# Routing pieces of an attention and mixture-of-experts kernel: spread over more steps, moved from VectorE to GpSimd, with GpSimd's row operations left at 128x1024

## The reference, cut to what matters

```
h = layernorm(x) * (1 + ca) + sa
x = x + ga * attention(h)                     # full softmax attention, rotary q and k
h = layernorm(x) * (1 + cb) + sb
logits = silu(h @ rw1 + rb1) @ rw2 + rb2      # the router: 8 logits per token
w = softmax over the two largest logits, 0 elsewhere
x = x + gb * (h + sum_e w[e] * (silu(h @ we1[e] + be1[e]) @ we2[e] + be2[e]))
```

## Time and profile before

| | us |
|---|---|
| median of 3 runs (lowest, highest) | 1129.0 (1128.48, 1135.22) |
| the profiled execution, its own time | 1136.76 |
| its span, first to last instruction | 1134.9 |
| busy in the span: PE, DVE, ACT, POOL | 922.2, 832.1, 730.0, 301.4 |
| granted TensorE clock, mean | 0.893 |

### The profile page before, as it was taken

How to read it: one execution, slowest core, us unless ns; L and a number is a source line. 1 busy time by engine, 2 the same in 40 slices (tenths; PEclk the granted TensorE clock), 3 DMA queues, 4 the chain that set the end, 5 groups by cost and what they waited for, 6 DMA issues and landing times. The chain is left out here.

```text
span 1134.9 us, 17714 instructions
## 1 busy us (share of the span) xinstructions
PE 922.2 (81%) x5990; PEld 370.1 (33%) x5990; DVE 832.1 (73%) x1159; ACT 730.0 (64%) x1576; POOL 301.4 (27%) x447
## 2 busy tenths in 40 slices
PE   2363569999998998999898999979978869987692
PEld 1232012222222222222222222312312159986682
DVE  3885989999998967999897789897682017443275
ACT  0033028888887875888687788869568846654361
POOL 1332000000001601400160330043023027677563
PEclk9666559999999987999899899989689989999896
DMA  4054430412420000160000110000000011122433
GB/s 121 0 211 165 152 127 1 155 55 102 155 96 33 29 2 34 34 196 29 2 29 5 43 48 2 28 13 18 2 19 20 1 39 58 58 67 66 129 112 106
DMA packets 57046, 72.67 MB, mean 64 GB/s; under 512 B 9504, under 2 KB 37664, under 8 KB 56960
## 3 DMA queue, kind: packets, MB, share of 16 engines
q1 hardware_dynamic: 52416, 62.21, 16.6%
q0 software_dynamic: 4544, 9.35, 2.3%
HBM read 30.08 MB, written 41.06 MB: 63 GB/s over the span
## 5 line engine op out<-in xcount | busy, mean ns | idle before, releaser
L847 DVE TENSOR_REDUCE half_max<-ps_max 128x2 f32<-128x1024 f32 x512 | 598.8, 1218 | 87.9 <-PE ps_max L667 85.2
L780 ACT ACTIVATE probs<-ps_scores 128x512 f32<-128x512 f32 x1024 | 538.7, 603 | 115.0 <-PE ps_scores L688 112.6
L701 PE MATMUL ps_ctx<-probs,v_grp 128*32 128x512 f32 x2048 | 289.2, 638 | 0.7 <-ACT probs L780 0.7
L688 PE MATMUL ps_scores<-q_set,k_set 51*128 51x512 bf16 x1024 | 260.3, 402 | 16.2 <-ACT probs L780 12.3
L667 PE MATMUL ps_max<-k_set,q_set 48*128 48x512 bf16 x1024 | 200.3, 418 | 83.4 <-DVE half_max L847 69.5
L688 PEld LDWEIGHTS ps_scores<-q_set,k_set 51*128 51x128 bf16 x1024 | 69.6, 94 | 335.0 <-ACT probs L780 305.9
L1423 ACT ACTIVATE hid<-ps_up,w_tile 128x128 f32<-128x128 f32 x312 | 89.0, 368 | 65.1 <-PE ps_up L1555 64.3
L612 POOL TENSOR_TENSOR ctx<-turned,inv_sum 128x128 f32<-128x128 f32 x32 | 12.9, 404 | 443.5 <-DVE inv_sum L870 443.5
L667 PEld LDWEIGHTS ps_max<-k_set,q_set 48*128 48x128 bf16 x1024 | 51.4, 97 | 196.6 <-DVE half_max L847 180.6
L1396 POOL DMA_INDIRECT y_rows<-y,y_to x78 | 95.0, 1218 | 21.7 <-POOL y_to L1393 21.7
L1555 PE MATMUL ps_up<-slots_t,w_tile 128*128 128x128 f32 x624 | 88.5, 287 | 12.0 <-DVE w_tile L1451 11.6
(11 more groups left out here) (171 smaller groups left out, 638.8 us busy)
## 6 DMA issues: line engine op xcount, KB each, us to landing
slots<-zero_rows SPq DMA_DIRECT2D x43, 387.0 KB, 5.9
q_terms<-parts SPq DMA_DIRECT2D x24, 256.0 KB, 2.7
k_terms<-parts SPq DMA_DIRECT2D x24, 256.0 KB, 3.0
q_set<-q_terms SPq DMA_DIRECT2D x32, 192.0 KB
k_set<-k_terms SPq DMA_DIRECT2D x32, 192.0 KB
slots_in<-slots SPq DMA_DIRECT2D x78, 64.5 KB, 1.8
rows<-y_rows SPq DMA_DIRECT2D x16, 256.0 KB, 4.1
w_all<-in_we SPq DMA_DIRECT2D x1, 2048.0 KB, 10.8
```

Of the source, the lines that this page charges most:

```text
L688: pe.matmul(bank[:], k_set[g % SETS][operand, u, tile * P:(tile + 1) * P], q_set[g % SETS][operand, u, c * BANK:(c + 1) * BANK], start=Tru ...
L701: ins = pe.matmul(ps_ctx[32 * head:32 * head + 32, :], v_grp[g % 2][:, tile, head, :], probs[:, s % RING, head, :], start=tile == 0, stop= ...
L780: act.activation(probs[:, s % RING, place, :], ps_scores[n % BANKS_S][:], ACT.Exp, scale=float(HD) ** -0.5).then_inc(slot_taken, 1)
L847: dve.reduce_max(half_max[g % 2][:, c, 2 * u:2 * u + 2, tile], ps_max[n % 2][:].rearrange("p (r n) -> p r n", r=2), axis=AX.X).then_inc(ma ...
```

## The change

The PE pieces of batches 0 to 2 are spread over n = 0 to 41 and the rest follows them. The logits are made in two halves. In `attend` ACT no longer uses Silu: it writes tanh(z/2) and z, POOL multiplies and adds (`silu`), and the logits are halved when they are copied. The counts are two matmuls over 96 columns, one with `before` and one with `ones`, and the running sum over the tiles of a batch is made by three shifted additions (`slots`). `slots` and `weights` move to POOL in `attend` (in `mix` they stay on DVE, in the new form). `tiles(0)` moves from n = 31 to n = 48. Row operations get a `parts` argument; it is 1 in both places, so POOL's row operations stay whole. In `mix` y_to is computed two tiles ahead, there are 8 instead of 4 y buffers, and the expert's number is loaded ahead of `add_bias`.

```diff
-YRING = 4
+YRING = 8
+PAD = 4
-ROUTE_AT = dict(zip(ROUTE, (0, 1, 2, 3, 17, 18, 20, 20, 22, 27)))
+ROUTE_AT = dict(zip(ROUTE, (0, 2, 5, 8, 21, 24, 26, 29, 32, 34, 41)))   # logits0, logits1, counts at the end
...
 # POOL in attend
-                    if n == 4:
+                    if n == 10:
                         pool.wait_ge(slot_taken, SLOT["proj1", b] + 1)
                         rows.gate(b)
                         rows.residual(b)
-                    if n == 9:
+                    if n == 14:
                         route.scale(b)
-                    if n == 10:
                         rows.norm(b, 0)
                         rows.norm(b, 1)
                         rows.modulate(b)
                         rows.shift(b)
-                    if n == 16:
+                    if n == 23:
                         rows.update(b)
-                    if n == 32:
+                    for half in range(2):
+                        if n == ROUTE_AT[f"router{half}"] + 1:
+                            pool.wait_ge(slot_taken, SLOT[f"router{half}", b] + 1)
+                            route.silu(half)
+                    if n == 42:
+                        pool.wait_ge(slot_taken, SLOT["counts", b] + 1)
+                        places.slots(b, 0)
+                    if n == 44:
...
                         route.scatter(b, 0, range(NT))
-                    if n == 39:
+                        places.weights(b)
+                    if n == 48:
                         route.destinations(b, 1)
...
 # PE and ACT in attend
+                if what in ("logits0", "logits1"):
+                    pe.wait_ge(r.act_ready, 4 * b + 2 * (int(what[-1]) + 1))
...
+                if what == "router0":
+                    act.wait_ge(r.x2_ready, b + 1)
...
 # DVE in attend
-                    if n == 7:
+                    if n == 13:
                         route.stats(b)
-                    if n == 8:
                         route.variance(b)
-                    if n == 24:
-                        dve.wait_ge(slot_taken, SLOT["logits", b] + 1)
+                    if n == 35:
+                        dve.wait_ge(slot_taken, SLOT["logits1", b] + 1)
...
                         route.first_choice()
-                    if n == 25:
+                    if n == 37:
                         route.second_choice()
-                    if n == 29:
-                        dve.wait_ge(slot_taken, SLOT["counts", b] + 1)
-                        route.slots(b, 0)
-                    if n == 30:
-                        route.weights(b)
-                    if n == 31 and b == EARLY - 1:
+                    if n == 48 and b == EARLY - 1:
+                        dve.wait_ge(r.slot_ready, EARLY)
                         route.tiles(0)
...
-            route.start_rooms()
...
 # route_rows; residual, modulate, shift and update in the same way
     def gate(b):
-        link(eng.tensor_tensor(r.gated[:], r.attn[:], mod(b, 2), ALU.mult))
+        by_parts(lambda at: eng.tensor_tensor(r.gated[:, at], r.attn[:, at], mod(b, 2, at), ALU.mult))
...
 # route_on_pool, tables: three more memsets, rb1_half, and next_slot set beside first_slot (16 more memsets)
+    def silu(half):
+        for i in range(2):
+            at = slice(half * BANK + i * BANK // 2, half * BANK + (i + 1) * BANK // 2)
+            pool.tensor_tensor(r.router_act[:, at], r.router_act[:, at], r.router_in[:, at],
+                               ALU.mult).then_inc(r.pool_step, 1)
+        pool.wait_ge(r.pool_step, r.pool_steps.more(2))
...  (the same two slices again, with ALU.add)
 # route_on_act; own_silu is False in attend, True in mix
-            return act.activation(r.router_act[:, columns], bank[:], ACT.Silu, bias=r.rb1[:])
+            if own_silu:
+                return act.activation(r.router_act[:, columns], bank[:], ACT.Silu, bias=r.rb1[:])
+            act.activation(r.router_act[:, columns], bank[:], ACT.Tanh, bias=r.rb1_half[:], scale=0.5)
+            return act.activation(r.router_in[:, columns], bank[:], ACT.Identity, bias=r.rb1[:])
...
 # route_places(eng, ...): POOL in attend, DVE in mix
+    def total(out, of, f4, f2):
+        link(eng.tensor_tensor(f4, of[..., 0:4], of[..., 4:8], ALU.add))
+        link(eng.tensor_tensor(f2, f4[..., 0:2], f4[..., 2:4], ALU.add))
+        link(eng.tensor_tensor(out, f2[..., 0], f2[..., 1], ALU.add))
+    def slots(b, stage):
+        room = r.next_slot[stage]
+        before, of, back = r.counted[:, 0, PAD:], r.counted[:, 1], 1
+        for run in r.run:
+            link(eng.tensor_tensor(run[:, PAD:], of[:, PAD:], of[:, PAD - back:PAD + NT - back], ALU.add))
+            of, back = run[:], 2 * back
+        link(eng.tensor_tensor(r.place_in[:], before, of[:, PAD - 1:PAD + NT - 1], ALU.add))
...  (then as before, with total() in place of each tensor_reduce)
 # route_on_pe
+            n = (PAD + NT) * NE
+            both = r.both[:].rearrange("p t e -> p (t e)")
+            pe.matmul(bank[:, 0:n], r.before[:], both, start=True, stop=True)
+            return pe.matmul(bank[:, n:2 * n], r.ones[:], both, start=True, stop=True)
...
 # POOL in mix
+            def address(n):
+                pool.wait_ge(slots_loaded[n % QRING], 16 * (n // QRING + 1))
+                if n >= YRING:
+                    pool.wait_ge(y_out[n % YRING], 16 * (n // YRING))
                 pool.tensor_scalar(y_to[n % YRING][:], slots_in[n % QRING][:, D:], float(n % YRING), None,
                                    ALU.max).then_inc(y_to_ready, 1)
+            def send(n):
                 pool.wait_ge(y_to_ready, n + 1)
+                pool.wait_ge(y_ready, n + 1)
...
 # DVE in mix
+                    e = expert(later)
                 add_bias(n)
-                if n + WRING - 1 < ALL_TILES:
-                    copy_w(n + WRING - 1)
+                if later < ALL_TILES:
+                    copy_w(later, e)
```

More of the change, by code:

```diff
@@ L74 @@
 assert CLEARS * CLEAR == SLOT_TILES
-ROUTE = ("ctx0", "ctx1", "proj0", "proj1", "turn0", "turn1", "router0", "router1", "logits", "counts")
+PAD = 4
+ROUTE = ("ctx0", "ctx1", "proj0", "proj1", "turn0", "turn1", "router0", "router1", "logits0", "logits1", "counts")
 class Count:
@@ L1082, in scatter @@
                                     r.h[:, i, :], None).then_inc(r.scattered, 16)
+    def silu(half):
[4 more added lines that the diff above has]
+        pool.wait_ge(r.pool_step, r.pool_steps.more(2))
+        for i in range(2):
+            at = slice(half * BANK + i * BANK // 2, half * BANK + (i + 1) * BANK // 2)
+            pool.tensor_tensor(r.router_act[:, at], r.router_act[:, at], r.router_in[:, at],
+                               ALU.add).then_inc(r.act_ready, 1)
     steps = Steps()
+    steps.silu = silu
     steps.tables = tables
@@ L1119, in route_on_act, with route_places, link, weights @@
     return steps
+def route_places(eng, k, r, step, steps):
+    wide = [P, NT, NE]
+    def link(ins):
+        ins.then_inc(step, 1)
+        eng.wait_ge(step, steps.more())
+    def total(out, of, f4, f2):
[5 more added lines that the diff above has]
+        before, of, back = r.counted[:, 0, PAD:], r.counted[:, 1], 1
+        for run in r.run:
+            link(eng.tensor_tensor(run[:, PAD:], of[:, PAD:], of[:, PAD - back:PAD + NT - back], ALU.add))
+            of, back = run[:], 2 * back
+        link(eng.tensor_tensor(r.place_in[:], before, of[:, PAD - 1:PAD + NT - 1], ALU.add))
+        link(eng.tensor_tensor(r.place_all[:], r.place_in[:], room[:].unsqueeze(1).to_broadcast(wide), ALU.add))
+        eng.tensor_tensor(room[:], room[:], of[:, PAD + NT - 1], ALU.add).then_inc(step, 1)
+        for n in range(2):
+            eng.tensor_tensor(r.place_of[:, n], r.chosen[:, n], r.place_all[:], ALU.mult).then_inc(step, 1)
+        eng.wait_ge(step, steps.more(3))
+        for n in range(2):
+            total(r.place[:, n], r.place_of[:, n], r.fold4[:, n], r.fold2[:, n])
+        eng.tensor_copy(r.slot[:, b], r.place[:]).then_inc(r.slot_ready, 1)
+    def weights(b):
+        eng.wait_ge(r.tanh_ready, b + 1)
+        eng.tensor_scalar(r.weight[:, b, 0, :], r.tanh_gap[:], 0.5, 0.5, ALU.mult, ALU.add).then_inc(step, 1)
+        eng.tensor_scalar(r.weight[:, b, 1, :], r.tanh_gap[:], -0.5, 0.5, ALU.mult, ALU.add).then_inc(step, 1)
+        eng.wait_ge(step, steps.more(2))
+    made = Steps()
+    made.slots = slots
+    made.weights = weights
+    return made
 def route_on_dve(dve, k, r):
-    wide = [P, NT, NE]
     step, steps = r.dve_step, r.dve_steps
-    def over_e(v):
-        return v[:].unsqueeze(2).to_broadcast(wide)
     def link(ins):
@@ L1133, in link @@
         dve.wait_ge(step, steps.more())
-    def start_rooms():
-        for stage in range(2):
-            dve.tensor_copy(r.next_slot[stage][:], r.first_slot[stage][:]).then_inc(step, 1)
-        dve.wait_ge(step, steps.more(2))
     def stats(b):
@@ L1233, in route_on_pe @@
 def route_on_pe(pe, k, r):
```

(5 more changed lines are left out.)

185 lines of the change are left out of this document (92 added, 93 removed).

## The result

The changed kernel takes 1117.47 us (median of 4 runs, 1113.29 to 1119.28), beside 1128.74 for the kernel before on the same chip. The ratio is 0.9882, with a 95% interval of 0.9836 to 0.9929. The direction is the predicted one; the size is not: 1.2% instead of 3.4%, and 1117 lies outside the range. The profiled execution took 1118.25 us with a span of 1116.4. Against the profiled span before, that is 18.5 us less where 38.2 were forecast. Up to the last exp 22.5 us were saved, of 37.2 forecast; the mix stage got 3.9 us longer where 1.0 less was forecast.

What follows compares the result with a forecast made beforehand. In undisturbed steps the PE-ACT loop and DVE's maxima were both closed at about 2.39 us. Three batches -32.9, tiles(0) -5, start +0.7 and mix -1.0 sum to -38.2 us: 1129.0 to 1091, range 1075 to 1109.

Steps and rivals of the forecast that it cites:

- Routers, counts, table loads: Routed batches: router halves save 1.75 us a batch, counts 6.1; no table load between the first exp and the last.
- The logits' halves: Logits in two halves beside the maxima, 0.5 us of delay each: -2.95 us a batch, -2.0 at the other end.
- The collision comes back: At DVE's step 21, two small DVE operations beside POOL's update take about 2.1 us each, as beside gate before.
- Change -0.2: Moving gate and residual removes 4.2 us a batch, 4.0 come back beside update; the difference was left out.
- Statistics and variance keep their price; two steps become one: DVE's routing work in a batch: doing both in one step leaves their cost unchanged.
- The choices stay on DVE, the same operations at the same price: DVE's choices beside the counts in a routed batch: no change in their cost.
- The mix stage: Counts -1.5 us, slots +0.7, register load +2, POOL's stretch -0.5, last y_to -1.7: sum -1.0, bounds -7 and +6.
- The slots: In mix: seven more operations on DVE at 0.18 us each, half of it covered: +0.7 us.
- the second: Stalls in routed batches move rather than vanish: +5.6 us a batch, 17 in all, giving 1108; chance 0.17.
- The first (no collision): POOL gets to update at another time, so DVE's split isn't stretched: a further 12 us, giving 1079; chance 0.13.
- third (Identity loads tables): On ACT, Identity is not in exp's table set; each router half loads two tables: 15 us, giving 1106; chance 0.04.
- fourth (POOL the bound): POOL holds PE at turn0 and makes the kernel slower: 1154 if it needs three times as long; chance 0.02.

## Why the prediction was right or wrong

- **Routers, counts, table loads**: right. The two router halves cost some 3 us (steps n = 26 to 32 take 18.05 us, less six of 2.39 and 0.7 for the turned context), 2.3 forecast; the counts cost two gaps of some 0.5. The logits' halves took 1.0 us each (11.55 us for four steps of 2.39) instead of 0.5, the other end of their bounds.
- **The collision comes back**: right in time, place and length (2.11 and 2.38 us for a forecast of about 2.1 each). **"Change -0.2" was wrong**: in the kernel before it cost 4.0 us, in the changed one 6.5 to 7.8. DVE is held as long as before, 4.1 us, but PE's clock falls behind it, where turn1 and the routers follow; at n = 4 the clock was low while DVE itself was held. That this makes the difference was not tested by itself.
- **"Statistics and variance keep their price; two steps become one"** failed. Joined behind an inversion they cost 3.1 to 3.4 us a batch more than apart in the profiled execution, more than their own work; 0.8 of it comes in every execution, the rest with the clock.
- **"The choices stay on DVE, the same operations at the same price"** failed for batches 0 and 1: 2.7 us each, since the second choice now stands behind the split of n = 37; 0.4 of it without the clock.
- These three steps are one mistake: DVE's work was counted by its sum, and the state after at the full clock. Corrected, they are 2.5 + 3.1 + 2.7 = 8.3 us in batch 0 and 2.6 + 3.3 + 2.7 = 8.6 in batch 1, where the shortfall was 7.3 and 7.4 (4.9 and 2.3 us saved for 12.2 and 9.7). Batch 2, with `tiles(0)`, was only 2.1 short although two of the blocks cost 3.8 + 3.4 us there, because the kernel before had lost more in it than I took: the step with `tiles(0)` alone took 8.9 us, 6.5 more than an undisturbed one, for 5.05 in the sum. The start was 1.4 us shorter and not 0.7 longer; over the profiles of kernels with the same start it varies by 2.8 us, so that is chance.
- **Without them the sum was good**: 192.3 - 12.2 is 180.1, less 4.2 for the collision is 175.9; with the three blocks resolved a batch took 175.1. That it fits so well is in part luck: routers, logits and counts cost 2.0 us more than I took, so some 2.8 us came back in places that I had not priced.
- **The mix stage**: forecast -1.0, measured +3.9. The counts gave their 1.5 us (tile 27: 3.45 to 1.97). The register load cost 1.9, as forecast (2), but most of it at the tail. The slots were mis-sized: forecast +0.7 with half of it covered, measured +2.0. They have eight operations more and not seven, each link takes 0.20 to 0.26 us with its wait, and none is covered. These three make +2.4. The other 1.5 us were put at nothing. With the register load back, the y of tile 26 still comes 1.8 us later behind that of tile 0 than in the kernel before; it is lost in tiles 7 to 25, mostly where DVE does the fourth batch's row work. There residual, shift and update now wait for their own end before they release others (`by_parts`, then `sem_inc`), which is a likely cause that no run tested. The tail's 1.7 us did not show in the changed kernel, where the last y is followed by 20.0 us as before, but only because the register load hid them: without it 18.8 us follow.
- **Rivals**: the second had the mechanism in its words "PE's clock falls behind the collision", but charged it to routers, logits and counts. Routers and counts stayed below its price, and only the logits cost the double as it said; its 1108 was short by 9. The first (no collision), third (Identity loads tables) and fourth (POOL the bound) are excluded by the rows above. POOL reached update in time.

## What to carry to other kernels

Where one engine is just fast enough for PE, price its extra work by the longest block, not by the sum: 2.3 us in one piece cost 4.4, in two pieces 1.2. Give such a block two prices, without and with a stretch at the low clock behind it (here 0.8 and 3.1 to 3.4 us more than apart), since one profile shows only one of them. After such a block look at the granted clock of the stretch behind it, and charge the state after the change with it as well as the state before. Where DVE itself was held during the stretch, as at n = 4 of the kernel before, it cost nothing more. And before cutting GpSimd's operations into pieces, try one wait that keeps a whole one away from VectorE's short SBUF operations; here it did the same.

## What the runs showed of the hardware

Beside POOL's 128x1024 operations a CAST of 128x32 took 2.38 us and a SCALAR_TENSOR_TENSOR 2.11, against 0.18 and 0.19 alone, and each ended within 0.04 us of POOL's operation. The Trainium skill, page "SBUF — State Buffer", section "SBUF: two separate sides", says that VectorE and GpSimd share one pair of ports by an exclusive lock that is held for a whole instruction; by that, the trace agrees.

A table load took 1.28 us, and a detour of two loads and a Silu left 0.05 us beside them. The Trainium skill, page "ScalarE: Activation LUTs", section "What ACT_TABLE_LOAD costs", adds a drain of about the same length to each switch, which no row here shows.

With this kernel 6.8 us at 1.2 GHz cost 2.3 to 2.6 us where DVE had to wait for PE, and the same block was followed by no such stretch, by 3.4 or by 6.8 us of it in different executions. And the same kernel, the one before, took 1128 to 1135 us in the earlier comparisons and 1162 to 1184 in the later ones, on three other chips, with PE's clock at 1.2 GHz in stretches that kept it full before. Whether that is the chips or the time at which they ran can't be told apart here: no chip is on record both early and late.
